# Moving 32 output columns from the plain part of a projection into its two seven-product column groups

## The reference, cut to what matters

```python
y = einsum('bsi,boi->bso', x, cond_weight[ids])            # 1024 -> 1024, weight chosen per element
base_out = einsum('btd,od->bto', y, base_W) + base_b       # 1024 -> 1024, same weight for all elements
probs = softmax(y @ router_W.T + router_b)                 # 15 routes, top 8 kept, mapped onto 8 experts
h = einsum('btd,erd->bter', y, A)                          # 8 experts x rank 16 = 128 columns
lora = einsum('bter,eor->bto', h * w[..., None], B) * 2.0
out = x + base_out + lora
```

## Time and profile before

| | |
|---|---|
| median of 3 runs | 404.79 us |
| the profiled execution | 404.47 us, its span 402.7 us |
| PE busy | 395.6 us, 98% |
| DVE busy | 306.3 us, 76% |
| ACT busy | 157.0 us, 39% |
| one element in the steady part (PE's first matmul of one to that of the next) | 48.10 us |

### The profile page before, as it was taken

The page is one execution under the profiler, slowest core; times in us unless marked ns, Lnnn a source line. Parts: engine busy times, 40 slices in busy tenths (PEclk is TensorE's granted clock), DMA queues, the critical chain, the costliest instruction groups (busy, mean ns, idle before and its releaser), DMA issues.

```text
span 402.7 us, 5975 instructions
## 1 busy us (share of the span) xinstructions
PE 395.6 (98%) x2102; PEld 348.9 (87%) x2102; DVE 306.3 (76%) x564; ACT 157.0 (39%) x223; POOL 2.0 (0%) x10
## 2 busy tenths in 40 slices
PE   6999999999999999999999999999999999999996
PEld 6888888888888888889888888888888898888885
DVE  2669999879978985688748896589856899468763
ACT  3658342663136421564025530265304642144300
POOL 0000001000000000000000000000000000000000
PEclk9999999999999999999999999999999999999999
DMA  7999106840268305573066520775026830464002
GB/s 287 396 392 399 48 0 208 278 144 0 104 221 300 105 0 174 190 260 104 0 208 226 213 81 0 260 256 200 13 68 245 292 125 0 138 225 161 2 0 104
DMA packets 25693, 64.71 MB, mean 161 GB/s; under 512 B 3410, under 2 KB 12626, under 8 KB 25682
## 3 DMA queue, kind: packets, MB, share of 16 engines
q1 hardware_dynamic: 25106, 62.47, 43.6%
q10 hardware_dynamic: 288, 1.05, 0.8%
q0 software_dynamic: 288, 1.05, 0.7%
HBM read 56.18 MB, written 8.39 MB: 160 GB/s over the span
## 4 chain that ended last, share of the span: by engine, by line
PE 86%; DVE 8%; ACT 2%; DMA 2%; issue 1%; SPq 0%; DVEq 0%
PE y_ps L836 26%; PE y_ps L838 13%; PE pl_ps L861 6%; PE x_ps L872 6%; PE x_ps L871 6%; PE x_ps L873 6%; PE s_ps L871 5%; PE s_ps L872 5%; PE s_ps L873 5%; PE pl_ps L862 3%; PE y_ps L849 2%; DMA w_raw<-in_wT 1%; DVE w_lo L509 1%; DVE res L618 1%; PE s_ps L886 1%; PE s_ps L888 1%
## 5 line engine op out<-in xcount | busy, mean ns | idle before, releaser
L836 PE MATMUL y_ps<-x_split,w_hi 128*128 128x512 f32 x496 | 173.4, 393 | 0.5 <-DVE y_sum L527 0.5
L838 PE MATMUL y_ps<-x_split,w_lo 128*128 128x256 f32 x496 | 138.9, 280 | 0.0
L836 PEld LDWEIGHTS y_ps<-x_split,w_hi 128*128 128x128 f32 x496 | 92.8, 187 | 22.0 <-DVE w_lo L509 1.1
L838 PEld LDWEIGHTS y_ps<-x_split,w_lo 128*128 128x128 f32 x496 | 93.7, 189 | 0.4
L385 ACT CAST w_hi<-w_raw 128x1024 fp32r<-128x1024 f32 x58 | 60.8, 1050 | 77.2 <-DMA w_raw<-in_wT 77.1
L509 DVE TENSOR_TENSOR w_lo<-w_raw,w_hi 128x1024 fp32r<-128x1024 f32 x58 | 70.9, 1224 | 19.5 <-ACT w_hi L385 17.9
L377 ACT COPY y_sum<-y_ps 128x256 f32<-128x256 f32 x62 | 23.0, 371 | 59.6 <-PE y_ps L838 59.6
L861 PE MATMUL pl_ps<-pl_split,y_hi 128*128 128x480 f32 x128 | 42.7, 383 | 0.0
L618 DVE TENSOR_TENSOR res<-x_ps,res 128x464 f32<-128x464 f32 (+1 forms) x30 | 19.5, 651 | 27.2 <-PE x_ps L888 15.1
L527 DVE TENSOR_TENSOR y_sum<-y_ps,y_sum 128x256 f32<-128x256 f32 x62 | 26.0, 420 | 15.2 <-ACT y_sum L377 15.0
L862 PE MATMUL pl_ps<-pl_split,y_lo 128*128 128x240 f32 x128 | 34.9, 273 | 0.0
(11 more groups left out here) (111 smaller groups left out, 536.2 us busy)
## 6 DMA issues: line engine op xcount, KB each, us to landing
w_raw<-in_wT SPq DMA_DIRECT2D x60, 512.0 KB, 3.6
res<-in_x SPq DMA_DIRECT2D x16, 512.0 KB, 4.7
x_raw<-in_xT SPq DMA_DIRECT2D x14, 512.0 KB, 4.8
out<-res SPq DMA_DIRECT2D x13, 512.0 KB, 3.1
early_raw<-in_wT SPq DMA_DIRECT2D x4, 512.0 KB, 9.1
hi_raw<-in_base_t SPq DMA_DIRECT2D x2, 928.0 KB, 9.7
st_raw<-in_base_t SPq DMA_DIRECT2D x2, 928.0 KB, 10.8
x_raw<-in_xT ACTq DMA_DIRECT2D x2, 512.0 KB, 4.4
```

The source lines that it names most:

```text
L836: nc.tensor.matmul(y_ps[:, c % 2, :], w_hi[:, s, k, :], x_split[:, k, :, :].rearrange("p s t -> p (s t)"), start=(k == 0), stop=False)
L838: mm = nc.tensor.matmul(y_ps[:, c % 2, 0:T], w_lo[:, s, k, :], x_split[:, k, 0, :], start=False, stop=(k == KC - 1))
```

## The change

```diff
@@ -46,7 +46,7 @@
     AR = ER + NR + 1
     KH = KC // 2
 
-    NP = 96
+    NP = 64
     NH = (D - NP) // 2
     PL = AR + NP
     DH = D // 2
```

## The result

The changed kernel takes 407.70 us (median of five runs) against 404.28 for the kernel before: ratio 1.0076, interval 1.0046 to 1.0106, slower by 3.1 us (3.4 by the medians). Forecast were +1.27 us and 406.0; the range ended at 407.2. Slower was right, the size was not. What follows is read from the profile of e1, the same kernel: 407.17 us, span 405.3.

What follows compares the result with a forecast made beforehand. PE's matmul slots were taken as the bound, with DVE and ACT in element 1. Elements 0 and 1 (+0.50) and 2 to 7 (+0.77) sum to +1.27 us, 406.0 us against 404.79; range 404.3 to 407.2.

Steps and rivals of the forecast that it cites:

- What bounds the kernel: All elements: PE's matmul slots set the time; only in element 1 do DVE and ACT set it.
- The price of product columns: Product matmuls gain 16 columns at 0.40 ns each: +6.4 ns a matmul, +0.54 us an element over 84.
- Rival 2: Product matmuls of 480 columns cost 0.220 us, +9.7 ns each; sum +3.2 us, 408.0 us; chance 0.08.
- The plain part: Plain matmuls: L861's 64 fewer columns save 25.6 ns each, -0.41 us an element; L862 counts as nothing.
- the load's floor: L862 in the plain part: its weight load keeps the slot at 0.109 us, so it returns 1 ns at most.
- Elements 0 and 1: First two elements: longer DVE and ACT work delays PE, giving +0.50 us together, +0.46 of it in element 1.
- The standstill of 0.65 us in element 1: Before the product with B11: PE's wait for DVE and ACT grows from 0.31 to about 0.65 us.
- Elements 2 to 7: Steady elements: products +0.54 less plain part 0.41, +0.13 us each, +0.77 together, with no other engine involved.
- Rival 1: Plain part: no floor under L862, slot 0.097 us; sum -0.2 us, 404.6 us; chance 0.17.
- rival 3: Plain part: a floor near 0.103 us gives L862 7 ns, 0.11 us an element; 405.3 us; chance 0.10.

Runs made afterwards that it cites:

- e1: The changed kernel measured once more, nothing else altered; 409.19 us median, ratio 1.0126 to the kernel before.
- e2: Kernel before with only L862 narrowed, to the first 208 of its 240 columns; 403.8 us, ratio 0.9997.
- g1: Changed kernel with all products of elements 1 to 7 at 464 columns except the last, kept at 480; 404.1 us, ratio 0.9990.
- e13: Kernel before with the last two pieces of stage 2 exchanged, the low-rank part ahead of the last product; 406.3 us, ratio 1.0060.
- f4: Changed kernel with all its SBUF buffers placed 832 bytes further on; 408.2 us.
- f1: Changed kernel with PE's loop starting at element 2 and element 1 written out ahead of it; 408.4 us.
- f2: Kernel before with PE's loop starting at element 2 and element 1 written out ahead of it; 404.8 us.
- e5: Changed kernel with the plain part's matmuls moved back to 480 and 240 columns; 411.5 us, ratio 1.0182.
- e6: Kernel before with the plain part's matmuls at 416 and 208 columns (480 for k = 0 in the wide one); 401.7 us, ratio 0.9928.
- e7: Changed kernel with one extra 128-column matmul ahead of each chunk 0 in elements 1 to 7; 409.3 us.
- f3: Changed kernel with one extra 256-column matmul ahead of each chunk 0; 408.5 us.
- e12: Kernel before with products of elements 2 to 7 at 480 columns and PE's loop starting at element 2; 409.6 us, ratio 1.0124.
- e4: The same edit with NP = 112 (products 456, L861 512, L862 256 columns), against the kernel before; 404.7 us, ratio 1.0013.
- e3: The same edit with NP = 80 (products 472, L861 448, L862 224 columns), against the kernel before; 405.0 us, ratio 1.0017.

## Why the prediction was wrong

**What bounds the kernel.** Right for the steady elements: PE's slots add up to the element there in every trace. Element 1 has the bound that was named. Element 2 has one that was not: in the kernel before DVE holds PE up by 0.06 us in it (below).

**The price of product columns.** The right mechanism, slightly small: 7.85/36 = 0.2181 against 0.2103, +7.8 ns for the +6.4 taken. Over 84 matmuls that is +0.66 for +0.54 (the low-rank part did not change its share by more than the last digit). Rival 2 named +9.7.

**The plain part.** The sum of both edits was -0.48 for -0.41. L862 under the load's floor was right in its effect and e2 shows it alone, 4 ns a pair where the columns would give 13 and the prediction took 1; the prediction looked for it in L862's slot, which reads 0.10, while the load spacing of 0.11 puts it into L861's. The pair gave back 30 ns in all, so 26 are left for L861's 64 columns, for 25.6.

**Elements 0 and 1.** Right: +0.50 forecast; from the first pair of element 0 to that of element 2 the changed kernel takes 109.84 - 14.21 = 95.63 against 110.40 - 15.33 = 95.07, +0.56. The standstill of 0.65 us in element 1 was hit, and the end of it, at the product with B11, came 0.39 us later after the first pair than before, where 0.04 and 0.31 were forecast.

**Elements 2 to 7: the step that failed.** The prediction had "No other engine comes in" and counted the 64 stage-1 pairs of each element at what they took before. They took 0.41 more an element: over elements 3 to 7 2.1 us, and in element 2 0.15 (22.60 for 22.45), since there the kernel before itself falls out of the fast rhythm half way. Its trace shows where, at the first matmul of chunk 4, shown with 0.45:

```profile
121.38 0.28 PE L838 MATMUL y_ps<-x_split,w_lo 128*128 128x256 f32 x1
121.50 0.45 PE L836 MATMUL y_ps<-x_split,w_hi 128*128 128x512 f32 x1
121.79 0.28 PE L838 MATMUL y_ps<-x_split,w_lo 128*128 128x256 f32 x1
```

Before it a pair takes 347 ns, after it 353, to the end of that stage 1; elements 2 to 4 are 48.37, 48.09 and 48.10 long. The slot of 0.29 holds 0.06 of standstill: DVE's y_sum (L527, 120.92 and 0.42 long) ended at 121.34 and the weight load behind it started at 121.45, as it did 0.11 after another L527 at the standstill before 69.52. The first two chunks of element 1 ran slow as well, with no standstill ahead of them. The prediction names neither and did not ask why the same matmuls had two prices in one trace. That question would have shown that there are two rhythms, not to which side the edit would move them.

Sum of the measured steps between the first pairs and the ends of the two profiles: elements 0 and 1 +0.56, element 2 +0.27 (48.65 for 48.37, before rounding), elements 3 to 6 4 x 0.59 = +2.4, element 7 with the end +0.6: 3.8 us. Of that 1.27 were forecast, 2.2 are the rhythm of the pairs (5 x 0.41 and 0.15), and the rest is product columns dearer and plain columns cheaper than taken. The spans differ by 2.6, because this execution's first pair began 1.1 us earlier; the medians differ by 3.1 to 3.4.

**The rivals.** Rival 2's figure of 408.0 was near the measured time by luck: it wanted +9.7 ns on the products, where 7.8 were measured, and most of the excess lies in stage 1. Rival 1 is refuted by e2. The 4 ns of e2 lie between the forecast's 1 and rival 3's 7. No rival named the stage-1 pairs.

**What stays open.** Why a pair has two rhythms, and what in the stream just ahead selects one. Shown is, for the steady elements, that the width of the last product does in the changed layout (g1, g2), that its place does in the old one (e13), and that a uniform shift (f4), the loop (f1, f2) and the plain part's width (e5, e6) do not. One extra matmul at the start left the pairs of the steady elements at 353 ns (e7, f3) but took those of element 1 from 347 to 353. All of it fits a rhythm that hangs on how the stream enters, to a few ns; that reading is argued and not shown. e12, 480 columns from blocks 1856 bytes apart and fast, leaves the spacing of the operands as a candidate for what shifts the entry; it was not tried alone.

## What to carry to other kernels

A stream of matmuls that alternates in width can have more than one steady pace, and an edit elsewhere can move it from one to the other; when a kernel is bound by such a stream, compare the slots of the untouched matmuls first, and look in one's own trace for the same loop at two prices. Read narrow matmuls in pairs with their neighbours: below the spacing of the weight loads (0.11 us here) most of the saving only moves into the neighbour's slot. And a change that gains by few columns (1344 added, 1536 removed here) must be priced per instruction with its floor: by the sum of columns an element would have got 0.08 us shorter, and with its rhythm left alone it gets 0.18 longer.

## What the runs showed of the hardware

- The same 64 pairs of 512 and 256 columns took 22.19 or 22.60 us, at a granted clock of 1.00 in both; a pace once begun held to the end of the stage unless a late matmul broke it (a slot of 0.29 us for 0.23 at 121.50 in the kernel before). The plain pairs of e4, of the same widths, show the same two paces (5.55 and 5.66 us for 16).
- Weight loads of 128x128 follow each other no closer than 0.11 us (107 ns is the least in any of these traces); the next load starts with the matmul before it or, when that matmul's own slot is under 0.11 us, behind its start (228.81 and 228.92 in e2), and the wide matmul after it shows the delay.
- float32r matmuls of 208, 224, 240 and 256 columns showed no jump in price: the plain pairs took 0.300 us (416 and 208), 0.313 (448 and 224, e3), 0.330 (480 and 240), and 0.347 for 512 and 256 (e4).
